# The sine products of the rotary embedding on VectorE: two operations for each projected piece in place of four

## The chip, the cores and the metric

The kernel runs on one core of a Trainium2 chip. A core has a matrix engine (TensorE, PE in the profile), a vector engine (VectorE, DVE), a scalar engine (ScalarE, ACT), GpSimd (POOL) and a queue that issues transfers (SyncE, SP). Each takes its instructions in order, and they wait for each other through semaphores. The metric is the device time of one execution in microseconds; the median of the runs counts.

## The reference

One macaron block on x of shape (8, 512, 512): half a feed-forward part, attention, half a feed-forward part, each on a layer-normalised input and added to x.

```python
x = x + 0.5 * ffn(layernorm(x), router_w, router_b, expert_w, expert_b)
x = x + attn(layernorm(x), Wq, Wk, Wv, Wo, lq1, lq2, lk1, lk2, rms_w)
x = x + 0.5 * ffn(layernorm(x), router_w, router_b, expert_w, expert_b)
# attn: 16 heads of q and 4 of k with 64 values (two halves of 32), v with 32
q = rope(q); k = rope(k)         # re*cos - im*sin, re*sin + im*cos, all 32 pairs of a head
energy = einsum('bqhad,bkhad->bahqk', q, k)      # a: the two halves, causal mask
scores = softmax(energy / sqrt(32))
diff = softmax(scores[:, 0] - lam * scores[:, 1])
att = einsum('bhqv,bvhd->bqhd', diff, v)         # then an rms norm and Wo
# ffn: each of 16 experts takes its 256 best tokens, weighted by the router's softmax
```

## The kernel before

The 4096 rows of x are 32 tiles of 128 rows. The program has three stages: the first feed-forward part (up to about 188 us), the middle with attention (to about 1745 us), and the choice of tokens of the second feed-forward part with the last sum. The change touches only the middle.

In the middle, three kinds of work run side by side. **Preparation** of a tile normalises its rows, turns them, projects them onto q, k and v in three pieces (`project(0)` and `project(1)`, 512 columns of q each, `project(2)`, 256 columns of k and 128 of v), rotates each piece (rope), splits it into two float16 parts and turns these for the energies. **Attention** handles pairs of a head and two row tiles: TensorE computes energies (L1923, mask L1925), VectorE takes each row's bias (`row_bias`, L1214), ScalarE exponentiates (L1670) with row sums, VectorE and GpSimd form the scaled difference (`inv_sums` L1221, `gamma` L1228, `mask` L1510, `scale` L1517, `difference` L1240, `diff_bias` L1249), GpSimd and ScalarE shift it (L1524, L1679), TensorE turns it (`turn_diff`, L1937), ScalarE exponentiates it (`probs`, L1687) and TensorE multiplies it with v (`weigh`, L1955), after which VectorE takes the head's result out (`take_head`, L1260). **After-work** on a tile takes the squares and sums of the heads (GpSimd L1621; VectorE `head_sums`, L1360 to L1367; GpSimd's power `head_root`, L1627), normalises (`head_norm`, L1373), multiplies with Wo and the experts' matrix and stores.

One turn of the middle's loop covers 8 pairs. The first 5 tiles are prepared in a prologue without attention; turns 0 to 26 then prepare tiles 5 to 31, the first five of these (to about 500 us) without after-work; the last five turns (from about 1433 us) have no preparation. `run_bodies` lays the order of each engine out from a table of slots: each turn has 24, three to a step. VectorE does `rope(0)` in slot 5, `rope(1)` in slot 9, `rope(2)` in slot 15; other work of the same engine stands before and behind it in a fixed order.

Rotating one piece is done by `rotate(n, ...)`. The weights' columns were laid out beforehand so that a head of 64 columns is `(a r f)`: two halves `a` of 32, in each 16 real parts and then 16 imaginary parts (`r`), `f` counting them. One operation (L1329) multiplies the piece in PSUM by the cosines into `rot`; four more (L1337), one for each `r` and `a`, multiply the other part of the same half by the signed sines into `rot_t`, which is the tile `scratch`. The last of the four raises `rope_v`. GpSimd waits for it and adds the two (`rope_add`, L1585); ScalarE takes the high float16 part (`rope_high`, L1715), GpSimd the low one (`rope_low`, L1600). TensorE waits for `rope_v` too, before it projects the next piece into the same bank. In the prologue the same `rotate` works on other buffers (`ex`, `df`, `pr`), and the adding is L1556.

Of the kernel before, what the change touches and what calls it, by code (L numbers as in the profile page):

```python
# [15 lines left out]
ALU = mybir.AluOpType  # L16
# [9 lines left out]
P = 128  # L26
B, S, E = 8, 512, 512
H, KVH = 16, 4
D = E // H
# [155 lines left out]
def program(nc, x, wqkv, wo, we, wr, lams, rms, rb, eb, consts, out, x1_d, x2_d, y2_d):  # L185
# [14 lines left out]
    with top:  # L200
# [714 lines left out]
        with ExitStack() as ctx:  # L915
# [285 lines left out]
            def _(dve):  # L1201
# [102 lines left out]
                def first_rope(u, n):  # L1304
                    if u >= 2:
                        rlo_done.wait(dve, 3 * (u - 2) + n)
                    proj_done.wait(dve, 3 * u + n)
                    rotate(n, p_bank(u, n), p_rot[u % 2][n], p_tmp[u % 2][n], u % TB)
# [14 lines left out]
                def rotate(n, bank_, rot_, tmp_, t):  # L1323
                    width = 512 if n < 2 else NK
                    heads = width // (2 * D)
                    src = bank_[:, 0:width]
                    cos = cst[:, ds(t * (2 * D) + C_COS, 2 * D)]
                    sin = cst[:, ds(t * (2 * D) + C_SIN, 2 * D)]
                    dve.tensor_tensor(rot_.rearrange("p (h f) -> p h f", h=heads),  # L1329
                                      src.rearrange("p (h f) -> p h f", h=heads),  # L1330
                                      cos.unsqueeze(1).broadcast_to([P, heads, 2 * D]), ALU.mult)
                    s4 = src.rearrange("p (h a r f) -> p h a r f", h=heads, a=2, r=2)
                    o4 = tmp_.rearrange("p (h a r f) -> p h a r f", h=heads, a=2, r=2)
                    n4 = sin.rearrange("p (a r f) -> p a r f", a=2, r=2)
                    for r in range(2):
                        for a in range(2):
                            ins = dve.tensor_tensor(  # L1337
                                o4[:, :, a, r, :], s4[:, :, a, 1 - r, :],
                                n4[:, a, r, :].unsqueeze(1).broadcast_to([P, heads, D // 2]), ALU.mult)
                    ins.then_inc(rope_v.sem, 1)  # L1340

                def rope(n):

                    width = 512 if n < 2 else NK

                    def f(u, pi):
                        if u is None:
                            return
                        if pi is not None:
                            ss_done.wait(dve, pi)  # L1350
                            dve.wait_ge(y2_st, pi * 16 + 16)
                        proj_done.wait(dve, 3 * u + n)
                        rlo_done.wait(dve, 3 * u + n - 1)
                        rotate(n, project_bank(n), rot[:, 0:width], rot_t[:, 0:width], u & 3)
                    return f
# [901 lines left out]
```

## Time and profile before

| | us |
|---|---|
| median of 3 runs | 1824.33 (1821.73 to 1828.74) |
| the profiled execution | 1832.2 |
| its span, from first to last instruction | 1830.4 |

| engine | busy us | share of the span |
|---|---|---|
| TensorE (matmul) | 1465.6 | 80% |
| VectorE | 1454.8 | 79% |
| ScalarE | 1261.2 | 69% |
| GpSimd | 1084.6 | 59% |

Busy time is a union over overlapping instructions. An instruction's own duration runs from its start to its end, and the next of the same engine may start before that end; so the distance between two starts says what the engine gives to an instruction, and the duration says more than that. The idle time in front of an instruction stands in brackets with what ended it. The profiled execution is 7.9 us above the median of the runs, 0.4%.

### The profile page before, as it was taken

The numbers are of one execution on the slowest core, as the hardware profiler recorded it, in microseconds if no ns is written. First come the engines' busy times: TensorE is split into PE (matmuls) and PEld (weight loads), VectorE is DVE, ScalarE is ACT, GpSimd is POOL, SyncE is SP. The second block draws the span as 40 slices with busy tenths as digits, with TensorE's granted clock in tenths as the row PEclk, the third lists the DMA queues.
The fourth block names the chain that finished last, engine by engine and source line by source line (L and its number), as shares of the span: only waits on it lengthen the run. The fifth ranks groups of instructions, "written<-read, shape, count | busy, mean of one in ns | idle before, by whom it ended". The sixth has DMA issues, their size and how long they took to land. (4 is left out here: it accounts for less than half of the span.)

```text
span 1830.4 us, 43823 instructions
## 1 busy us (share of the span) xinstructions
PE 1465.6 (80%) x10688; PEld 1028.4 (56%) x10688; DVE 1454.8 (79%) x5505; ACT 1261.2 (69%) x3426; POOL 1084.6 (59%) x1493
## 2 busy tenths in 40 slices
PE   3996735988889898988888988888888888888620
PEld 3542313766666666666666666666666666566310
DVE  6778416888898888889988888888989877684477
ACT  2362325787788788878888888878878777675320
POOL 5421534666677777777777777777767666554300
PEclk9998866788899999989999999899989977886855
DMA  8024221111111111111111111111111100001186
GB/s 305 2 64 151 83 68 32 35 36 32 30 46 45 50 44 50 44 44 47 48 44 44 44 44 44 44 44 50 49 45 50 47 22 17 17 23 41 41 314 251
DMA packets 178954, 115.99 MB, mean 63 GB/s; under 512 B 139090, under 2 KB 139474, under 8 KB 178899
## 3 DMA queue, kind: packets, MB, share of 16 engines
q1 hardware_dynamic: 178898, 115.34, 21.4%
q8 instruction: 25, 0.41, 0.1%
q14 instruction: 31, 0.25, 0.0%
HBM read 50.26 MB, written 33.55 MB: 46 GB/s over the span
## 5 line engine op out<-in xcount | busy, mean ns | idle before, releaser
L1670 ACT ACTIVATE ex<-bank,nbias 128x512 f32<-128x512 f32 (+3 forms) x1024 | 528.8, 540 | 80.9 <-DVE bank L1214 78.6
L1214 DVE TENSOR_SCALAR_CACHE_REDUCE bank<-bank,nesc 128x512 f32<-128x512 f32 (+3 forms) x1024 | 503.2, 551 | 88.8 <-PE bank L1925 88.1
L1955 PEld LDWEIGHTS bank<-vs,pr 128*128 128x128 f32 x2560 | 332.8, 205 | 24.3 <-issue 12.3
L1955 PE MATMUL bank<-vs,pr 128*128 (+1 forms) x2560 | 337.6, 283 | 10.2 <-DVE att L1260 5.7
L1937 PE MATMUL bank<-cst,df 128*128 128x128 f32 x1280 | 264.6, 309 | 85.9 <-ACT pr L1687 85.2
L1923 PE MATMUL bank<-ks,hall 96*128 (+2 forms) x1024 | 266.7, 337 | 71.5 <-ACT ex L1670 48.1
L1517 POOL TENSOR_SCALAR ex<-ex,gam 128x128 f32<-128x128 f32 (+3 forms) x512 | 318.7, 635 | 0.0
L1687 ACT ACTIVATE pr<-bank 128x128 f32<-128x128 f32 (+3 forms) x512 | 232.3, 454 | 87.9 <-PE bank L1937 86.8
L1240 DVE CUSTOM_DVE_ANT_0 df<-ex 128x128 f32<-128x128 f32 (+3 forms) x512 | 261.3, 525 | 8.5 <-issue 4.0
L1937 PEld LDWEIGHTS bank<-cst,df 128*128 128x128 f32 x1280 | 168.4, 166 | 114.4 <-ACT pr L1687 99.0
L1670 ACT ACTIVATION_READ_ACCUMULATOR ex<-bank,nbias 128x1 f32 x1024 | 223.8, 219 | 0.0
L1925 PE MATMUL bank<-mask_b,ident_b 128*128 128x128 bf16 x1024 | 210.4, 239 | 0.0
L1923 PEld LDWEIGHTS bank<-ks,hall 96*128 (+1 forms) x1024 | 111.0, 108 | 164.6 <-issue 99.8
L1679 ACT ACTIVATE df<-df,dbias,rsum 128x512 f32<-128x512 f32 (+1 forms) x256 | 201.8, 788 | 0.0
L1524 POOL TENSOR_SCALAR df<-df,rsum,dbias 128x128 f32<-128x128 f32 (+1 forms) x256 | 147.7, 577 | 38.7 <-DVE dbias L1249 38.7
L1600 POOL TENSOR_TENSOR split<-rot,split 128x512 f16<-128x512 f32 (+1 forms) x81 | 80.6, 995 | 112.6 <-ACT split L1715 112.6
L238 PE MATMUL bank<-wqkv_h,b_xt 128*128 128x512 f16 x360 | 142.3, 395 | 3.2 <-ACT turned L1757 1.2
L240 PE MATMUL bank<-wqkv_h,b_xt 128*128 128x512 f16 x360 | 143.6, 399 | 0.0
L239 PE MATMUL bank<-wqkv_l,b_xt 128*128 128x512 f16 x360 | 143.0, 397 | 0.0
L1214 DVE DVE_READ_ACCUMULATOR bank<-bank,nesc 128x1 f32 x1024 | 140.7, 137 | 0.0
L1228 DVE SCALAR_TENSOR_TENSOR gam<-esum,lam,rsum 128x2 f32<-128x2 f32 x256 | 113.6, 444 | 33.7 <-DVE rsum L1221 23.9
L1510 POOL TENSOR_SCALAR_AFFINE_SELECT ex<-ex 128x256 f32<-128x256 f32 x256 | 122.2, 477 | 22.2 <-DVE gam L1228 22.2
(358 smaller groups left out, 2942.1 us busy)
## 6 DMA issues: line engine op xcount, KB each, us to landing
hall<-turned SPq DMA_DIRECT2D x360, 64.0 KB, 2.1
x_dram<-hall SPq DMA_DIRECT2D x8, 1024.0 KB, 4.9
hall<-x_dram SPq DMA_DIRECT2D x8, 1024.0 KB, 14.5
c_y<-y_dram SPq DMA_DIRECT2D x8, 1024.0 KB, 14.5
out_dram<-hall SPq DMA_DIRECT2D x8, 1024.0 KB, 4.7
hall<-in_x SPq DMA_DIRECT2D x7, 1024.0 KB, 13.8
x<-x_dram SPq DMA_DIRECT2D x28, 256.0 KB, 2.7
x_dram<-x SPq DMA_DIRECT2D x28, 256.0 KB, 2.0
```

The source lines that it names most:

```text
L240: mm = eng.matmul(acc, a_lo(k), b_hi(k), start=False, stop=last and k == KT - 1)
L1214: dve.tensor_scalar(part, part, nesc[:, 0:1], None, ALU.mult, ALU.min, accum_out=nbias[:, j, i, a:a + 1]).then_inc(bias_done.sem, 1)
L1240: dve.tensor_tensor_reduce(out=df[j % 4][:, lo:hi], in0=ex[j % 4][:, 0, lo:hi], in1=ex[j % 4][:, 1, lo:hi], scale=1.0, scalar=-3e38, op0=A ...
L1517: gp.tensor_scalar(ex[j % 4][:, 1, lo:hi], ex[j % 4][:, 1, lo:hi], gam[:, j, i:i + 1], 1.0, ALU.mult, ALU.mult).then_inc(scaled.sem, 1)
L1524: gp.tensor_scalar(df[j % 4][:, lo:hi], df[j % 4][:, lo:hi], rsum[:, j, 0, 0:1], dbias[:, j, 0:1], ALU.mult, ALU.add).then_inc(shifted_sho ...
L1670: ac.activation(ex[j % 4][:, a, lo:hi], energy(j, i)[:, a, :], ACT.Exp, bias=nbias[:, j, i, a:a + 1], scale=-1.0, accum_out=esum[:, j, i, ...
L1679: ac.activation(df[j % 4][:, lo:hi], df[j % 4][:, lo:hi], ACT.Identity, bias=dbias[:, j, 1:2], scale=rsum[:, j, 1, 0:1]).then_inc(shifted_ ...
L1687: ac.activation(pr[j % 2][:, lo:hi], bank[:, 6, 0:hi - lo], ACT.Exp).then_inc(prob_done.sem, 1)
L1923: pe.matmul(out_e, q.rearrange("p a n -> p (a n)"), k.rearrange("p a n -> p (a n)"), start=True, stop=True)
L1925: mm = pe.matmul(out_e[:, n - P:n], ident_b[:, :], mask_b[:, :], start=False, stop=True, skip_group_check=True)
L1937: tr = pe.transpose(bank[:, 6, k * P:(k + 1) * P], df[j % 4][:, lo + k * P:lo + (k + 1) * P], ident)
L1955: mm = pe.matmul(bank[:, 7, t * DV:(t + 1) * DV], pr[j % 2][:, lo + k * P:lo + (k + 1) * P], val, start=(k == 0), stop=(k == t))
```

## The change

For each `r` there was one operation for half `a` = 0 and one for `a` = 1. Now one operation takes both: its output and its first input keep the dimension of the halves, and the sines are read as (heads, 2, 16), repeated over the heads.

```diff
                     for r in range(2):
-                        for a in range(2):
-                            ins = dve.tensor_tensor(
-                                o4[:, :, a, r, :], s4[:, :, a, 1 - r, :],
-                                n4[:, a, r, :].unsqueeze(1).broadcast_to([P, heads, D // 2]), ALU.mult)
+                        ins = dve.tensor_tensor(
+                            o4[:, :, :, r, :], s4[:, :, :, 1 - r, :],
+                            n4[:, :, r, :].unsqueeze(1).broadcast_to([P, heads, 2, D // 2]), ALU.mult)
                     ins.then_inc(rope_v.sem, 1)
```

With 8 heads in a piece an operation now has 256 elements for each partition where it had 128; with 4 heads it has 128 where it had 64. Every other instruction stays where it stood in its engine's order. The lines behind L1337 move up by one.

## Rows read from the trace of the kernel before

**Rows 1.** Page, 40 equal slices of the span: busy tenths of two engines.
```profile
PE   3996735988889898988888988888888888888620
...
DVE  6778416888898888889988888888989877684477
```

**Rows 2.** Busy time by stretch: length; PE, PEld, DVE, ACT, POOL; clock, DMA.
```profile
525.30:1405.54 880.24, 788.69 (x6019) 565.68 (x6017) 782.99 (x3063) 729.39 (x2042) 647.14 (x901) 0.93 0.18 46
790.16:834.71 44.55, 39.96 (x304) 28.29 (x303) 38.95 (x154) 36.52 (x103) 32.05 (x46) 0.92 0.19 46
834.71:877.42 42.71, 38.05 (x308) 27.75 (x307) 38.94 (x156) 36.42 (x103) 32.52 (x46) 0.99 0.19 48
```

**Rows 3.** Groups of VectorE by shape, whole span: busy, mean ns, idle before.
```profile
L1337 DVE TENSOR_TENSOR scratch<-bank,cst 128x128 f32<-128x128 f32 x216 | 46.8, 275 | 0.0
...
L1337 DVE TENSOR_TENSOR scratch<-bank,cst 128x64 f32<-128x64 f32 x108 | 16.3, 212 | 0.0
```

**Rows 4.** Timeline of VectorE around two pieces: start, duration, instruction.
```profile
913.63 0.42 DVE L1329 TENSOR_TENSOR rot<-bank,cst 128x256 f32<-128x256 f32 x1
913.97 0.61 DVE L1337 TENSOR_TENSOR scratch<-bank,cst 128x64 f32<-128x64 f32 x4
914.49 0.17 DVE L1221 RECIPROCAL rsum<-esum 128x4 f32<-128x4 f32 x1
...
938.58 0.87 DVE L1337 TENSOR_TENSOR scratch<-bank,cst 128x128 f32<-128x128 f32 x4
939.37 0.74 DVE L1214 TENSOR_SCALAR_CACHE_REDUCE bank<-bank,nesc 128x512 f32<-128x512 f32 x1
```

**Rows 5.** Waits between 525 and 1405 us: total, times, longest.
```profile
DVE bank L1214 <- PE bank L1925: 28.0, 20, 2.1
DVE att L1260 <- PE bank L1955: 25.2, 18, 3.0
...
POOL rot L1585 <- DVE scratch L1337: 35.2, 40, 2.1
```

**Rows 6.** Timeline of the turn from 965 us, rope(0) and what follows.
```profile
975.65 2.92 POOL L1627 TENSOR_TENSOR ast<-ast,half 128x16 f32<-128x16 f32 x1 [2.15 <-DVE ast L1367]
...
980.90 0.87 DVE L1337 TENSOR_TENSOR scratch<-bank,cst 128x128 f32<-128x128 f32 x4
...
984.29 1.27 POOL L1585 TENSOR_TENSOR rot<-rot,scratch 128x512 f32<-128x512 f32 x1
...
985.75 0.62 ACT L1715 CAST split<-rot 128x512 f16<-128x512 f32 x1 [0.90 <-POOL rot L1585]
```

**Rows 7.** The same turn, rope(1), then the next wait of VectorE.
```profile
988.81 0.86 DVE L1337 TENSOR_TENSOR scratch<-bank,cst 128x128 f32<-128x128 f32 x4
...
989.76 1.27 POOL L1585 TENSOR_TENSOR rot<-rot,scratch 128x512 f32<-128x512 f32 x1 [0.33 <-DVE scratch L1337]
...
999.73 0.62 DVE L1214 TENSOR_SCALAR_CACHE_REDUCE bank<-bank,nesc 128x384 f32<-128x384 f32 x1 [2.04 <-PE bank L1925]
```

**Rows 8.** The same turn, rope(2), then the next wait of VectorE.
```profile
1001.96 0.60 DVE L1337 TENSOR_TENSOR scratch<-bank,cst 128x64 f32<-128x64 f32 x4
...
1014.00 0.29 DVE L1260 COPY att<-bank 128x132 f32 x1 [0.87 <-PE bank L1955]
```

**Rows 9.** VectorE in an early turn, and around rope(2) of the turn from 834 us.
```profile
473.39 0.60 DVE L1337 TENSOR_TENSOR scratch<-bank,cst 128x64 f32<-128x64 f32 x4
...
867.93 0.63 DVE L1214 TENSOR_SCALAR_CACHE_REDUCE bank<-bank,nesc 128x384 f32<-128x384 f32 x1 [0.37 <-PE bank L1925]
...
870.15 0.61 DVE L1337 TENSOR_TENSOR scratch<-bank,cst 128x64 f32<-128x64 f32 x4
```

**Rows 10.** Timeline of TensorE in the turn from 965 us.
```profile
988.43 0.33 PE L1937 MATMUL bank<-cst,df 128*128 128x128 f32 x1 [0.50 <-ACT pr L1687]
...
995.79 0.33 PE L240 MATMUL bank<-wqkv_h,b_xt 128*128 128x384 f16 x1
...
996.42 0.53 PE L240 MATMUL bank<-wqkv_h,b_xt 128*128 128x384 f16 x1
```

## What the change does to the time: the prediction

> **What bounds the kernel now.** I read the slices of the page first. In the middle stage both TensorE and VectorE stand at 8 or 9 tenths busy, slice after slice [rows 1], so the slices do not say which of them sets the pace; a change that takes work from VectorE might give all of it or nothing. The busy time by stretch says the same: of 880.2 us that 20 full turns take, TensorE is busy 788.7 and VectorE 783.0 [rows 2]. A turn is 880.2 / 20 = 44.0 us.
>
> The next view is that of the waits in these turns. VectorE does wait: 28.0 us in 20 waits for energies in front of `row_bias`, and 25.2 us in 18 waits for the product with v in front of `take_head` [rows 5]. Both stand once in most turns. Two places a turn where VectorE sits idle until TensorE has something for it mean that time saved ahead of such a place only makes that wait longer, unless TensorE's work itself hung on what VectorE did faster. So the question is not how much VectorE saves but which of the sine products lie on the chain that sets a turn.
>
> For that I went back through a turn from each instruction to what ended last before it: the releaser in brackets where there was idle time, else the instruction in front. In the turn from 965 us the chain goes so: VectorE waits for `weigh`, takes the head out and goes on without a gap to the head sums; these release GpSimd's power L1627 at 975.65, after 2.15 us of idle time of GpSimd; GpSimd then works without a gap until `rope_add(0)` at 984.29, 1.27 us long; ScalarE waits 0.90 us for it [rows 6]; ScalarE's probabilities release TensorE's L1937 at 988.43 [rows 10]; TensorE's product with Wo, its energies, turns, another exchange with ScalarE and the third projection follow, up to the energies that VectorE awaits at 999.73 for 2.04 us [rows 7]. So each of the four engines holds a part of the turn, and VectorE's part is the stretch with the head sums and sometimes that behind 999.73.
>
> **The change part by part.** *What an operation gives back.* The four operations of a piece with 128 elements last 275 ns each by their own durations, those with 64 elements 212 ns [rows 3]. But their starts are closer: four of the larger begin at 938.58 and the next instruction at 939.37, 0.79 us or 0.198 us for one; four of the smaller take 914.49 - 913.97 = 0.52 us, 0.13 each [rows 4]. What VectorE gives to a piece is this distance. From 64 to 128 elements it grows by 0.068 us, or 1.06 ns for an element, and what is left for no elements at all is 0.062 us. Merging two operations saves that constant once.
>
> *What the new ones cost.* The trace of before has no operation of VectorE of just this form, with three dimensions in the sines and 256 elements. The nearest row is the cosine product of the third piece: 256 elements from PSUM, the cosines repeated over four heads; it starts at 913.63 and the next at 913.97, 0.34 us [rows 4]. Two of these are 0.68 us in place of 0.79: 0.11 us saved for a large piece. A small piece becomes two operations of 128 elements, 2 x 0.198 = 0.40 in place of 0.52: 0.12 us saved. I take these values, since rows of 16 elements with a jump between them are already in the old operations, at the same rate as the cosine's plain rows. The lower bound of the cost is the constant taken in full, 2 x 0.062 = 0.124 us saved for each. The upper bound, should a third dimension break the overlap with the next instruction, is the full duration of the cosine product, 0.42 us [rows 4]: 2 x 0.42 = 0.84 in place of 0.79, 0.05 us lost.
>
> There are 32 tiles with two large pieces and one small: 64 x 0.11 + 32 x 0.12 = 10.9 us less work for VectorE in all (from 12 us less to, by the upper bound, about 5 us more).
>
> The Trainium skill weighs an operation higher. In "VectorE: DVE Perf Modes", section "The TRN2 errata — SBUF-src ops pay a fixed extra latency per instruction", a VectorE operation from PSUM costs 120 cycles and one for each element at 0.96 GHz, and many small tiles pay the constant each time. By that estimate each operation left out gives back 125 ns, 250 ns for a piece and 24 us in all. The durations agree with such a constant (275 ns against 258 by the page), the distances between starts do not (62 ns); the same page's section "Two Vector instructions with no wait between them" says that an instruction that is not held starts before the one in front has ended, and the rows show that here. The sum goes by the distances.
>
> *rope(0).* In the full turns its sines start at 980.90 and are over about 0.8 us later. GpSimd, for which they are meant, gets to `rope_add(0)` only at 984.29, having worked without a gap since 975.65 [rows 6]. The sines are early by some 2.6 us, and 0.11 more is nothing. VectorE's own next steps gain 0.11, but run into operands that GpSimd delivers on the same late chain. On the path: 0.
>
> *rope(1).* Its sines do release GpSimd at 989.76 after a wait of 0.33, so `rope_add(1)` starts 0.11 us earlier. What comes of that: VectorE reaches the wait for energies earlier, 2.04 us long in this turn [rows 7], 0.37 in about a third of the turns [rows 9]. Both are longer than 0.11. ScalarE takes the sum up far later, in its own order. On the path: 0; the cover is that wait, and if it were gone this piece would bring 20 x 0.11 = 2.2 us.
>
> *rope(2).* It stands behind the wait for energies, so VectorE is on the path up to there in some turns. In the turn from 965 us it is not: a second wait of 0.87 at 1014.00 follows [rows 8], and TensorE and ScalarE got there by a chain of their own. In others it is: in the turn from 834 us the energies come at 867.93, the sines follow at 870.15 and VectorE goes on without a wait for TensorE to the next head sums [rows 9]. Following the chain back through all 20 turns I find the sines of rope(2) on it 7 times, those of the other two never.
>
> *The early turns and the prologue.* In the five turns without after-work the chain holds less of GpSimd, and 9 of their 15 pieces lie on it, the last at 473.39 [rows 9]; in the prologue one, since ScalarE, GpSimd and later the stacking transfers hold it up. The last five turns rotate nothing.
>
> *The sum.* 7 + 9 + 1 = 17 pieces on the path, 0.12 us each: 2.0 us. The profiled execution of 1832.2 us would become 1830.2; taken off the median of 1824.33, which is 7.9 us below the profiled one, it is 1822.3 us. Bounds of the operation's cost on these 17 pieces: 2.1 us faster to 0.9 us slower.
>
> **The rivals.** *All of VectorE's saving comes through.* VectorE is busy 783.0 of 880.2 us, in a turn at the full clock 38.94 of 42.71 [rows 2], and if it paced every turn the 10.9 us would all be gained: 1813.4 us. For it speaks that in the turns of 42.71 us VectorE waits least. Against it, the two waits for TensorE, 53.2 us in 20 turns, which this rival needs to be on a path that itself shortens.
>
> *The durations are the price.* If an operation's own duration counted, a large piece would go from 4 x 0.275 to 2 x 0.42 us and a small one from 4 x 0.212 to 2 x 0.275: 0.26 and 0.30 us saved, 26 us in all [rows 3, 4]. On the 17 pieces of the path that is 17 x 0.27 = 4.6 us, 1819.7 us; all through, 1798 us. Against it speak the starts in rows 4, in every piece. The Trainium skill's price from the section named above would give 17 x 0.25 = 4.3 us, or 24 us all through.
>
> *TensorE's clock, other side.* TensorE's matmuls in the third projection go from 0.33 to 0.53 us at about 996 us [rows 10], the step from the full clock to the half, and the turn from 790 us, with a mean granted clock of 0.92, takes 44.55 us where that from 834 us, at 0.99, takes 42.71 with the same work [rows 2]. Each turn has short half-clock stretches behind waits of TensorE; a few turns have fewer. The change shifts the instructions by a tenth of a microsecond against these stretches. If each of the 20 turns came out like that of 790 us, it would cost 20 x (44.55 - 44.01) = 10.8 us and use up the saving: 1835.1 us, slower. It decides in the third projection, from the point where TensorE's pause in front of it is followed by the half clock in every turn. *The same with luck:* each turn like the one from 834 us, 20 x (44.01 - 42.71) = 26 us, or 1798 us; half of the turns, 1811.
>
> *The merged operation is slow,* 0.42 us each: 17 x 0.05 = 0.9 us on the path, and at the very most 96 x 0.05 = 4.8 us: 1825 to 1829, no difference that can be seen.
>
> **How the numbers follow.** A measurement of this kernel can tell about 0.5%, 9.1 us, from no change: 1815.2 to 1833.5. Chances: the forecast, 0.71; the durations as the price, but off the path, 0.02; the slow merged operation, 0.05; all through, 0.09; the clock to the good, 0.06; the clock to the bad, 0.07. Faster by over 0.5% are the last but two and the last but one: 0.15. Slower: 0.07. Within: 0.78. The range takes in the first rival (1813) and part of the clock's good case, and reaches up to the spread of the runs of before (4.4 us above the median) and some of the clock's bad case: 1811 to 1832; what it leaves out, the ends of the two clock cases, is about 1 in 10.
>
> **What would show it.** In the profile after: two operations for a piece, about 0.34 us from start to start in the large ones and 0.20 in the small, and VectorE's busy time down by about 11 us; the wait for energies in front of `row_bias` and that in front of `take_head` together longer by about what VectorE saves in the full turns, some 5 us; GpSimd still without a gap from L1627 to `rope_add(0)`; turns of about 44 us, with a mean clock near 0.93. It would be wrong if VectorE's waits stayed as they were and the turns shrank by 0.3 us, or if the clock of the turns moved by some hundredths.

## The result: slower by 0.8% in the first measurement, by 0.3% over three

| | before | after |
|---|---|---|
| median of 4 runs each | 1823.88 us (1821.73 to 1828.74) | 1838.82 us (1835.47 to 1842.12) |
| ratio | | 1.0078, interval 1.005 to 1.0106 |
| profiled execution, its span | 1832.2, 1830.4 us | 1839.7, 1837.9 us |
| VectorE busy | 1454.8 us | 1441.9 us |

The forecast was 1822.3 us, a gain of 2 us too small to be seen, with 1811 to 1832 as its range; the measured median lies above the range, and the change is a small loss. Later sets of executions of the same two kernels give smaller losses: 1.0013 (0.9997 to 1.0028) with 12 of after and 29 of before, and 1.0033 (1.0014 to 1.0053) with 8 and 13. The interval of the first of these includes 1. All three sets together hold 24 executions of after with a mean of 1835.9 us and 46 of before with 1830.7: about 5 us or 0.3%, and 4 us without the first set. Not one of the 24 is below 1830 us; of before 20 of 46 are. The first four of before, with a mean of 1824.6 us, were all among the lower ones of their kind, and the first four of after, with 1838.8, lie above the mean of theirs; so the first measurement shows more than there is. The executions of before in all sets reach from 1819.8 to 1846.4 us, over 26 us, and what spreads them is the thing to explain.

What the change was to do to VectorE it did. The groups of VectorE by shape, whole span of the changed kernel (busy, mean ns, idle before; they answer to [rows 3]):

```profile
L1336 DVE TENSOR_TENSOR scratch<-bank,cst 128x256 f32<-128x256 f32 x108 | 39.9, 408 | 0.0
...
L1336 DVE TENSOR_TENSOR scratch<-bank,cst 128x128 f32<-128x128 f32 x54 | 12.8, 278 | 0.0
```

And its timeline around a large and a small piece (start, duration; they answer to [rows 4]):

```profile
1030.64 0.74 DVE L1336 TENSOR_TENSOR scratch<-bank,cst 128x256 f32<-128x256 f32 x2
1031.30 0.74 DVE L1214 TENSOR_SCALAR_CACHE_REDUCE bank<-bank,nesc 128x512 f32<-128x512 f32 x1
...
1050.01 0.48 DVE L1336 TENSOR_TENSOR scratch<-bank,cst 128x128 f32<-128x128 f32 x2
1050.40 0.17 DVE L1221 RECIPROCAL rsum<-esum 128x4 f32<-128x4 f32 x1
```

A large piece takes 0.66 us from start to start where it took 0.79, a small one 0.39 where it took 0.52. That is 0.13 us for either, 96 x 0.13 = 12.5 us in all, and VectorE's busy time fell by 12.9. The third dimension costs nothing that can be seen here, and over the 20 full turns no other group of VectorE takes more than 0.6 us longer than before.

The time was lost elsewhere. Busy time by stretch, one turn of the changed kernel, then all 20 full ones (length; PE, PEld, DVE, ACT, POOL; granted clock; they answer to [rows 2]):

```profile
1012.77:1057.14 44.37, 39.77 (x304) 28.11 (x303) 38.64 (x150) 36.37 (x103) 31.96 (x46) 0.92 0.18 46
525.13:1412.13 887.00, 794.82 (x6022) 562.72 (x6021) 773.11 (x2943) 727.36 (x2041) 640.07 (x901) 0.92 0.18 46
```

The full turns take 887.0 us in place of 880.2, which is nearly all of the 7.5 us between the two profiled spans. And nearly all of them are alike: from the fourth of the 20 on each takes 44.36 to 44.38 us. In the profile of before they varied from 42.71 [rows 2] to 44.71. TensorE's timeline shows where such a turn spends its clock; 16-bit matmuls of 512 columns in the experts' product of the changed kernel:

```profile
970.92 0.63 PE L238 MATMUL bank<-we_h,at 128*128 128x512 f16 x1
972.20 0.63 PE L238 MATMUL bank<-we_h,at 128*128 128x512 f16 x1
973.22 0.38 PE L238 MATMUL bank<-we_h,at 128*128 128x512 f16 x1
...
1045.51 0.33 PE L240 MATMUL bank<-wqkv_h,b_xt 128*128 128x384 f16 x1
```

Up to 972.2 they last 0.63 us, at half the clock (1.2 GHz), then 0.38, at the full one (2.4 GHz). In these turns the half-clock stretch lies at this place every time, and the third projection (the last line, from the next turn) runs at the full clock. In the turn of before from 965 us it is the other way round: the experts' product runs at the full clock, and the third projection falls to the half [rows 10].

```profile
968.28 0.38 PE L240 MATMUL bank<-we_h,at 128*128 128x512 f16 x1
```

In the changed kernel VectorE then waits for the product with v behind it, 2.98 us in the turn from 1012.77. Waits between 525 and 1412 us, which answer to [rows 5]:

```profile
DVE att L1260 <- PE bank L1954: 56.1, 20, 3.1
...
DVE bank L1214 <- PE bank L1924: 12.8, 20, 2.0
POOL rot L1584 <- DVE scratch L1336: 12.7, 40, 1.8
```

Two waits behind the experts' product grew with it. ScalarE waits for its result 34.6 us in 19 waits, before 7.9 in 5, and GpSimd for the transfer of that result out of `scratch` 38.5 us in 18 waits, before 9.0 in 5.

### The profile page after: what moved, and what is told of

The parts are those of the page before. It is cut to its first block and busy times, and to the rows that moved or that the text cites. A ratio compares the mean times of both kernels' runs of the same rounds, so it can differ in the third digit from the quotient of the medians.

```text
span 1837.9 us, 43581 instructions
## 1 busy us (share of the span) xinstructions
PE 1473.1 (80%) x10688; PEld 1025.9 (56%) x10688; DVE 1441.9 (78%) x5313; ACT 1259.1 (69%) x3426; POOL 1076.3 (59%) x1493
## 5 line engine op out<-in xcount | busy, mean ns | idle before, releaser
L1516 POOL TENSOR_SCALAR ex<-ex,gam 128x128 f32<-128x128 f32 (+3 forms) x512 | 314.6, 625 | 0.0
L1240 DVE CUSTOM_DVE_ANT_0 df<-ex 128x128 f32<-128x128 f32 (+3 forms) x512 | 256.9, 516 | 9.4 <-issue 4.9
L1669 ACT ACTIVATION_READ_ACCUMULATOR ex<-bank,nbias 128x1 f32 x1024 | 228.3, 223 | 0.0
L238 PE MATMUL bank<-wqkv_h,b_xt 128*128 128x512 f16 x360 | 137.9, 383 | 3.0 <-ACT turned L1756 1.2
L239 PE MATMUL bank<-wqkv_l,b_xt 128*128 128x512 f16 x360 | 138.4, 384 | 0.0
L240 PE MATMUL bank<-wqkv_h,b_xt 128*128 128x512 f16 x360 | 137.9, 383 | 0.0
L1509 POOL TENSOR_SCALAR_AFFINE_SELECT ex<-ex 128x256 f32<-128x256 f32 x256 | 118.2, 462 | 22.2 <-DVE gam L1228 22.2
## 6 DMA issues: line engine op xcount, KB each, us to landing
c_y<-y_dram SPq DMA_DIRECT2D x8, 1024.0 KB, 14.6
```

The costliest lines, as they stand in the source:

```text
L239: eng.matmul(acc, a_hi(k), b_lo(k), start=False, stop=False)
L1240: dve.tensor_tensor_reduce(out=df[j % 4][:, lo:hi], in0=ex[j % 4][:, 0, lo:hi], in1=ex[j % 4][:, 1, lo:hi], scale=1.0, scalar=-3e38, op0=A ...
L1516: gp.tensor_scalar(ex[j % 4][:, 1, lo:hi], ex[j % 4][:, 1, lo:hi], gam[:, j, i:i + 1], 1.0, ALU.mult, ALU.mult).then_inc(scaled.sem, 1)
L1669: ac.activation(ex[j % 4][:, a, lo:hi], energy(j, i)[:, a, :], ACT.Exp, bias=nbias[:, j, i, a:a + 1], scale=-1.0, accum_out=esum[:, j, i, ...
```

## The experiments

**Theory A**: what sets a full turn is whether and where TensorE falls to half its clock behind its waits; the change moves the kernel from a mixture of turns, some with hardly any time at half clock, to turns that always have a long stretch of it. **Theory B**: the merged operations meet GpSimd's otherwise and lengthen its chain, or are bad by their form.

### The kernel before once more, and one piece at a time

The unchanged kernel:

> The kernel before, unchanged, once more, for a second profile of it: the one profiled execution of before took 1832.2 us, 8 us above its median, so its pattern of turns may not be the usual one. Theory A (the turns are held at a fixed length by TensorE's half-clock stretch, and before escapes from that in some turns): the same time as before, near 1823 us, and in the profile more turns of about 42.7 us than the 2 of 20 of the first profile, and hardly any run of turns of 44.37 us. Theory B (the merged operations shift VectorE against GpSimd, and GpSimd's own chain gets longer by collisions): the full turns here are all alike and about 0.7 us shorter than the 44.37 us of the changed kernel.

Measured: median 1830.2 us of 10, from 1825.6 to 1839.6; ratio 1.0002 (0.998 to 1.0025). That is 7 us above the 1823 expected: the first executions of before had been unusually quick. Its profiled execution was a quick one, 1825.6 us. Five turns of it in a row, then the 20 full ones:

```profile
877.64:921.40 43.76, 39.01 (x299) 27.97 (x297) 39.66 (x154) 36.41 (x103) 32.36 (x46) 0.92 0.18 46
921.40:965.36 43.96, 39.48 (x302) 28.36 (x301) 39.12 (x154) 36.36 (x103) 31.95 (x46) 0.93 0.18 46
965.36:1009.60 44.24, 39.83 (x304) 28.64 (x303) 39.16 (x154) 36.60 (x103) 32.36 (x46) 0.92 0.18 46
1009.60:1053.43 43.83, 39.34 (x302) 28.28 (x301) 39.03 (x156) 36.23 (x103) 32.44 (x46) 0.93 0.18 46
1053.43:1096.09 42.66, 38.04 (x308) 27.77 (x307) 38.91 (x154) 36.41 (x103) 32.42 (x46) 0.99 0.19 48
528.92:1402.26 873.34, 782.32 (x6019) 563.74 (x6017) 783.74 (x3061) 728.24 (x2042) 646.15 (x901) 0.94 0.18 47
```

This pattern of five repeats through the whole stage, with four turns of 42.7 us, and the 20 turns take 873.3 us. The first profile of the kernel before had taken 880.2 with two such short turns. So one kernel, unchanged, has several patterns, and an execution falls into one of them: the two profiles of before lie 6.6 us apart, nearly as far as before and after.

For the three pieces the operations were merged in one of them only, in the loop, with the prologue as before:

```diff
-                    for r in range(2):
-                        for a in range(2):
+                    if not early and n == 0:          # 1 and 2 in the other two kernels
+                        for r in range(2):
+                            ...                       # one operation
+                    else:
+                        for r in range(2):
+                            for a in range(2):
```

> Of the change only the merged sines of the first piece, rope(0), in the loop; prologue and the other pieces as before. Its sines are over 2.6 us before GpSimd adds them. Theory A: any shift of a tenth of a microsecond may change the pattern, so each piece alone can come out anywhere between 1818 and 1840 us, with turns of 44.37 us wherever it is slow. Theory B: a piece that is early for GpSimd anyway does nothing, 1822 to 1825 us.

Measured: 1829.8 us (1823.6 to 1840.3), ratio 1.0003 (0.9982 to 1.0024); the profiled execution of 1840.3 us had its turns held at 44.37.

> Only rope(1) merged, in the loop. Theory A: between 1818 and 1840 us, slow only with turns of 44.37 us. Theory B: rope_add(1) starts 0.11 us earlier and may meet GpSimd and VectorE otherwise; if the loss comes from here alone, 1835 us or more, and the sum of the three pieces' effects is the whole change's 15 us.

Measured: 1830.9 us (1821.3 to 1834.6), ratio 1.0007 (0.9991 to 1.0024); the profiled execution of 1821.3 us had four of 20 turns below 43 us.

> Only rope(2) merged, in the loop. Theory A: between 1818 and 1840 us, slow only with turns of 44.37 us, and the three pieces' effects do not add up to the whole change's 15 us. Theory B: they add up; this one is the piece on the path in 7 of 20 turns, so 1 to 2 us faster if no collision comes of it.

Measured: 1830.6 us (1827.4 to 1835.2), ratio 1.0002 (0.9981 to 1.0023). None of the three can be told from the kernel before. That speaks against one piece that carries the 15 us of the first measurement; but each interval is some 4 us wide to either side, so a third of a loss of 5 us in each piece would not be seen. The runs also show that one profile of such a kernel says little: the three fell into three different patterns. One turn of each of the first two, at the same place:

```profile
1013.13:1057.49 44.36, 39.79 (x303) 28.12 (x302) 38.92 (x154) 36.38 (x103) 31.97 (x46) 0.92 0.18 46
```
```profile
963.42:1006.05 42.63, 38.01 (x308) 27.75 (x307) 38.79 (x152) 36.38 (x103) 32.39 (x46) 0.99 0.19 48
```

### More and less work for VectorE

The changed kernel again, beside many executions of before:

> The changed kernel, unchanged, once more beside many runs of the kernel before. Executions of before now spread from 1824 to 1841 us, and profiled ones show two patterns of turns: a held one (every turn 44.37 us, one long half-clock stretch in each) and a mixed one (42.7 to 44.2 us). Theory A1 (the change makes the held pattern more likely): the ratio stays near 1.008, and most executions lie at 1835 to 1842 us with a mean clock of 0.861 to 0.864. Theory A2 (the pattern is drawn anew in every execution, the first measurement of four runs drew badly): a ratio within 0.997 to 1.003, with executions from 1824 to 1842 us.

Measured: 1833.9 us of 12 (1830.8 to 1839.5), ratio 1.0013 (0.9997 to 1.0028), before 1823.9 to 1842.2. Between A1 and A2: the median is 3.4 us higher and the quick executions are missing. In its profile no turn of the 20 is below 43.97 us.

```diff
                     n4 = sin.rearrange("p (a r f) -> p a r f", a=2, r=2)
+                    dve.tensor_reduce(pad[:, n:n + 1], cst[:, 0:64], X, ALU.max)
```

> The merged sines, and before them in each piece one small operation of VectorE (a maximum over 64 constants, written to a tile that nobody reads) that gives back the 0.12 us saved. Nothing of the computation is left out. Theory A1, by timing: like the kernel before, ratio 1.000. If the form of the merged operation did harm by itself: like the changed kernel, 1.008. Theory A2: 1.000 within 0.3%.

Measured: 1831.7 us of 11 (1826.2 to 1845.1), ratio 0.9998 (0.9979 to 1.0018). With the time given back the quick executions are there again: 4 of 11 below 1830 us, where the changed kernel has none in 24. That speaks for the timing and against the form of the merged operation, though not alone: e6 and e5 lie 2 us apart, and their intervals overlap.

```diff
-                    for r in range(2):
+                    for r in range(parts):            # 1 in the loop, 2 in the prologue
```

> In the loop only the first of the two merged sine products of a piece; the other, half of the sine products, is left out (the tile is zeroed once, so that half of it holds old values). VectorE saves another 0.34 us for a large piece and 0.20 for a small one, 0.9 us a turn, three times what the change saves. If VectorE's work on these pieces were on the path, 27 turns x 1.2 us = 32 us faster than before; by the reading of the prediction (17 pieces on the path, 0.45 us) 7 us faster, 1816 to 1823 us against before's 1823 to 1830. Theory A1: any value down to 1815 or up to 1840 us, by the share of turns held at 44.37 us.

Measured: 1837.1 us (1830.1 to 1841.3), ratio 1.0027 (1.0011 to 1.0043). By the sum of the expectation VectorE has some 24 us less to do than in the changed kernel; the kernel is not faster than that one, and slower than before. Two of its turns:

```profile
877.94:922.44 44.50, 39.80 (x303) 28.64 (x302) 38.58 (x145) 36.55 (x103) 32.57 (x46) 0.92 0.18 46
922.44:966.64 44.20, 39.66 (x303) 28.54 (x302) 38.38 (x147) 36.44 (x103) 32.64 (x46) 0.92 0.18 46
```

These two lengths alternate for the most part, 44.2 and 44.5, with the clock at 0.92: a pattern of its own, without a short turn. That time saved on these pieces comes through as a whole is ruled out.

VectorE's busy time in a turn hardly fell (38.4 and 38.6 us against 38.8 in e5), though 0.9 us of work was gone. Groups of VectorE between 530 and 1400 us show why, in e5 and then in e7:

```profile
L1228 DVE SCALAR_TENSOR_TENSOR gam<-esum,lam,rsum 128x2 f32<-128x2 f32 x157 | 77.5, 493 | 24.1 <-DVE rsum L1221 18.7
...
L1240 DVE CUSTOM_DVE_ANT_0 df<-ex 128x384 f32<-128x384 f32 x79 | 46.4, 588 | 0.0
L1240 DVE CUSTOM_DVE_ANT_0 df<-ex 128x256 f32<-128x256 f32 x79 | 33.1, 419 | 3.5 <-issue 3.5
```
```profile
L1241 DVE CUSTOM_DVE_ANT_0 df<-ex 128x384 f32<-128x384 f32 x79 | 67.7, 856 | 0.0
...
L1229 DVE SCALAR_TENSOR_TENSOR gam<-esum,lam,rsum 128x2 f32<-128x2 f32 x157 | 54.3, 346 | 21.8 <-DVE rsum L1222 16.3
L1241 DVE CUSTOM_DVE_ANT_0 df<-ex 128x256 f32<-128x256 f32 x79 | 43.5, 550 | 3.5 <-issue 3.5
```

Between 530 and 1400 us the sine products take 17 us less. The differences take more, 0.86 us on average in place of 0.59 with 384 elements and 0.55 in place of 0.42 with 256, in all four lengths 33.5 us; gamma takes less, 0.35 in place of 0.49, 23.2 us in all. So 10 of the 17 us come back as longer instructions. Both kinds read two operands from SBUF. Gamma visibly lasts until GpSimd is done: in the turn of [rows 7] it ran from 989.91 to 991.04, GpSimd's addition from 989.76 to 991.03, and of gamma's 160 executions in the full turns of before all 42 that last over 0.6 us end with an instruction of GpSimd, to within 0.03 us. So part of the time that VectorE gains is spent inside a later instruction that lasts until GpSimd has finished, where it counts as busy. That the differences stretch for the same reason was not checked.

```diff
                     n4 = sin.rearrange("p (a r f) -> p a r f", a=2, r=2)
+                    dve.tensor_reduce(pad[:, 2 * n:2 * n + 1], cst[:, 0:64], X, ALU.max)
+                    dve.tensor_reduce(pad[:, 2 * n + 1:2 * n + 2], cst[:, 0:64], X, ALU.max)
```

> The kernel before with two small operations of VectorE more in each piece (maxima over 64 constants, written to a tile that nobody reads), about 0.25 us a piece, 0.75 us a turn. If VectorE were on the path: 27 x 0.75 = 20 us slower. By the reading of the prediction: 17 pieces x 0.25 = 4 us slower, since the waits for the energies and for the product with v take the rest. Theory A1: not in line with the sum, faster than before if the turns fall out of the held pattern.

Measured: 1846.3 us of 4 (1842.3 to 1851.5), ratio 1.009 (1.0068 to 1.0112). Slower, by 16 us where the reading by waits gave 4 and full exposure 20. In its profile, of 1842.3 us, the 20 full turns take 882.1 us, no more than in other executions; three of the early turns take 44.4 where they took 41.1 to 41.3, and the full turns start 14 us later than in the profile of before. One of these early turns, and its counterpart in the kernel before:

```profile
405.52:449.92 44.40, 40.83 (x250) 30.20 (x249) 34.72 (x150) 33.09 (x98) 26.18 (x41) 0.73 0.15 28
```
```profile
398.41:439.57 41.16, 35.03 (x251) 26.02 (x250) 34.14 (x146) 33.17 (x98) 26.00 (x41) 0.88 0.13 30
```

The time is lost where the clock is lost, 0.73 in place of 0.88, with VectorE only 0.6 us busier; so this run does not show what VectorE's work costs by itself.

### TensorE kept at work in front of its waits

The decisive test gives TensorE more to do. Behind the energies of each pair, and behind its product with v, come some short matmuls of constants into the PSUM bank that is free at that time; they lie in front of waits for ScalarE.

```diff
+                def keep_warm(j, count):
+                    free = (3, 2, 1, 0)[j % 4]
+                    for _ in range(count):
+                        pe.matmul(bank[:, free, 0:P], ident_b[:, :], ones_b[:, :], start=True, stop=True)
...
                         mm.then_inc(e_done.sem, 1)
+                        if i == 0:
+                            exp_done.wait(pe, at.units(4, -1))
+                            keep_warm(j, 4)
...
                     mm.then_inc(av_done.sem, 1)
+                    keep_warm(j, 4)
```

> The kernel before, with TensorE kept at work in front of its waits for ScalarE: four short matmuls of constants (128 columns) behind the energies of each pair and four behind its product with v, into a PSUM bank that is free there, 64 in a turn, about 3.5 us of TensorE's time by the 0.055 us that a matmul of 128 columns in 16 bits takes from start to start at the full clock; TensorE stands idle for 4.5 us of a turn. They change no result. Theory A (the turns are held near 44.4 us by half-clock stretches that follow TensorE's waits): the mean clock of the full turns rises from 0.92 to 0.97 or more and they get shorter, 43 us or less, in spite of more work for TensorE; 1800 to 1825 us. If the clock is only a bystander: TensorE's added work lengthens the turns by 1 to 3 us each, 1850 us or more.

Measured: 1796.9 us (1795.5 to 1798.8), ratio 0.9822 (0.9754 to 0.989); before 1825.6. More work for TensorE makes the kernel 29 us faster, more than expected. The matmuls came with one more wait of TensorE for ScalarE in each pair; e11 below has that wait too and no gain, so it is not the wait. One of its turns and all 20:

```profile
864.20:906.52 42.32, 39.78 (x365) 30.12 (x366) 39.41 (x156) 36.42 (x103) 32.36 (x46) 1.00 0.19 48
...
524.10:1372.11 848.01, 796.78 (x7290) 603.54 (x7309) 787.91 (x3061) 728.47 (x2041) 647.52 (x901) 1.00 0.19 48
```

> The same added matmuls in the changed kernel. Theory A: where the clock stays up, the merged sines are worth what the prediction said, 2 us less than the same matmuls in the kernel before (e9), at most 11; the difference between e9 and e10 is then no loss. If the merging does harm by itself, e10 is 3 to 15 us slower than e9.

Measured: 1801.3 us (1798.6 to 1805.5), ratio 0.985 (0.978 to 0.992). It is 4.3 us slower than e9, which by the expectation speaks for a harm of the merging by itself; its turns say what that harm is:

```profile
864.81:908.86 44.05, 41.22 (x374) 31.34 (x373) 39.08 (x150) 36.58 (x103) 31.96 (x46) 0.97 0.18 46
908.86:951.07 42.21, 39.74 (x367) 30.09 (x366) 39.05 (x150) 36.28 (x103) 32.36 (x46) 1.00 0.19 48
...
1035.46:1079.51 44.05, 41.22 (x373) 31.32 (x373) 39.07 (x148) 36.58 (x103) 31.96 (x46) 0.97 0.18 46
523.51:1376.76 853.25, 802.11 (x7284) 607.06 (x7302) 780.94 (x2941) 727.09 (x2041) 645.24 (x901) 0.99 0.19 48
```

This pair of runs shows the whole case in small. At the full clock a turn takes 42.20 us with the merged sines and 42.33 without: one piece's 0.13 us of the three does come through. But with them every fourth turn has a half-clock stretch and takes 44.05 us, 1.85 more. Three turns win 0.13 each, the fourth loses 1.7: over 20 turns 853.3 us against 848.0. A turn that is a tenth of a microsecond shorter meets the drops of the clock otherwise, and one drop costs fourteen times what the edit saves in a turn.

> The kernel before with two short matmuls at each of these places, 32 in a turn, 1.8 us of TensorE's time. Theory A: the clock rises less than with four (0.93 to 0.97), and the time lies between before and e9. If the clock is a bystander: half of e9's loss.

Measured: 1830.5 us (1825.8 to 1836.2), ratio 1.0016 (0.9978 to 1.0053). No gain, and neither the loss of a bystander clock nor the part of the gain that A expected: three of its full turns take 42.2 us, and the last 14 are held at 44.37 with a clock of 0.92. The changed kernel, e2 and e6 are held at the same length, with other work in the turn.

```profile
962.85:1007.22 44.37, 41.24 (x335) 30.07 (x334) 39.00 (x156) 36.40 (x103) 32.37 (x46) 0.92 0.18 46
```

> The kernel before with six short matmuls of constants at each of the two places of a pair, 96 in a turn, 5.3 us of TensorE's time. No half-clock stretch in the 20 full turns. The turns get longer than the 42.33 us with four where the matmuls no longer fit into TensorE's waits: 42.3 to 44 us, 1797 to 1830 us.

Measured: 1798.5 us (1796.7 to 1801.4), ratio 0.9818 (0.9767 to 0.9868). Two of the 20 full turns still hold a half-clock stretch and take 44.4 us, where none was expected; the others take 42.7 to 42.8.

> The same in the changed kernel. If the merged sines are worth their time wherever the clock stays up: no half-clock stretch in the full turns, each of them up to 0.13 us shorter than in e12, and 0 to 5 us less in all. If something else in the merged operations costs time: e13 slower than e12 by 2 us or more with the same clock.

Measured: 1787.5 us of 4 (1783.9 to 1794.9), ratio 0.9754 (0.9696 to 0.9811): the fastest kernel of the study, 45 us below before in the same set of runs, and 11 below e12, where 0 to 5 were expected. Turns of e12 and of e13:

```profile
736.09:778.83 42.74, 40.90 (x398) 31.81 (x398) 39.14 (x154) 36.31 (x103) 32.36 (x46) 1.00 0.18 48
```
```profile
729.42:772.16 42.74, 40.91 (x398) 31.84 (x398) 38.73 (x150) 36.28 (x104) 32.42 (x46) 1.00 0.19 48
```

At the full clock the turns are equal, 42.74 us; TensorE, busy 40.9 of them, now sets them, and the 0.4 us less of VectorE (39.14 and 38.73 busy) bring nothing. So the 11 us are not the saving in these turns. The two profiled executions lie 6.1 us apart: the early turns end 6.7 us earlier in e13, its full turns take 3.2 us longer, 861.5 against 858.3, since four of them hold a half-clock stretch where two do in e12, and what follows them is 3 us shorter. In turns at the full clock the merged sines do no harm, 42.74 against 42.74 here and 42.20 against 42.33 in e10 and e9; how much of the 11 us is the edit and how much the pattern of the stretches, four executions do not tell.

> The changed kernel with five matmuls at each place, between e10 and e13. By the clock alone: the half-clock stretch of every fourth turn in e10 is gone and the turns stay near 42.2 to 42.6 us, so 1792 to 1800 us, 3 to 8 us faster than e10. If one more matmul at each place costs more than it keeps: 1801 us or more.

Measured: 1798.2 us (1797.8 to 1800.5), ratio 0.9815 (0.9765 to 0.9865). As expected by the clock: one half-clock turn in 20, the others 42.45 us.

> The changed kernel with eight matmuls behind the energies of each pair and none behind its product with v: 64 in a turn as in e10, at one place in two. If the amount decides: turns and time as in e10, 1799 to 1805 us. If the place decides: half-clock stretches in most turns again, 1815 us or more.

Measured: 1827.9 us of 10 (1813.1 to 1837.3), ratio 0.9974 (0.9942 to 1.0005). The same 64 matmuls a turn as in e10, 27 us slower: the amount alone does not decide, the place does too. Of its 20 full turns eight take 42.7 to 42.95 us and twelve 44.33 to 44.38.

> The changed kernel once more, to settle the size of the loss. If the first measurement of four executions was a bad draw from the patterns of turns: a ratio of 1.000 to 1.003, as in e5, with a profiled execution whose turns of 42.7 us are few or none. If the loss is 15 us: 1.006 or more.

Measured: 1836.4 us of 8 (1831.7 to 1844.8), ratio 1.0033 (1.0014 to 1.0053), with one turn of 42.9 us in the profile. Smaller than the first measurement's 1.0078, larger than e5's and just above the 1.000 to 1.003 expected; the intervals of the first and of e5 do not meet, so an interval from a few executions of one set is narrower here than the kernel's own variety.

With this profile there are three of the changed kernel and two of the kernel before. The record of the granted clock in the traces, added up over the 20 full turns, gives this (us):

| profiled execution | the 20 full turns | of that at half clock | full turns less half of it |
|---|---|---|---|
| e1, kernel before | 873.3 | 108.8 | 818.9 |
| first profile of before | 880.2 | 122.4 | 819.0 |
| e16, changed kernel | 883.4 | 129.0 | 818.9 |
| e5, changed kernel | 886.8 | 135.8 | 818.9 |
| first profile of after | 887.0 | 136.1 | 819.0 |

Each microsecond at half clock costs half a microsecond, with the merged sines or without, and nothing else tells these five apart, to within 0.2 us: in the full turns the loss is half-clock time, and the saving for VectorE does not show. The kernels e2, e3, e4, e6, e7 and e8 give 818.1 to 820.0 in the last column. It is an account and not a forecast for a kernel without half-clock time: e9, with its added matmuls, has hardly any and takes 848.0.

Whole executions point the same way less sharply. In the 109 executions of before that have a mean granted clock on record, the time is 1.7 us longer for each 0.001 of clock less (correlation -0.88). The 24 of the changed kernel have a mean clock of 0.8658 against 0.8679, worth 3.5 of the 5.1 us between the two means; the other 1.6 us are not explained. And not all of the spread lies in the full turns: the profiled execution of e16, the slowest of the changed kernel at 1844.8 us, has the shortest full turns of its three and starts them 8.4 us later than the first profile of before.

## Why the prediction was wrong, step by step

- **Price of an operation: right.** 0.13 us a piece measured, 0.11 to 0.12 taken, 0.124 as the lower bound. VectorE's busy time fell by 12.9 us where 11 was said. The estimate of 250 ns a piece from the Trainium skill ("VectorE: DVE Perf Modes", section "The TRN2 errata — SBUF-src ops pay a fixed extra latency per instruction") was not seen.
- **What lies on the path: right in kind.** Of the three pieces of a turn at most one is on it: 0.13 us a turn in e9 against e10, where the prediction had 7 x 0.12 over 20 turns at the mixed clock. Without added matmuls even those 0.8 us do not show in the table above. e7 shows that three times the saving gains nothing either.
- **The waits in front of `row_bias` and `take_head`** grew together from 53.2 to 68.9 us, by 15.7, not by 5: VectorE's saving in 20 turns (20 x 3 x 0.13 = 8) and the 6.8 us by which the turns are longer make 14.6 of it. The prediction named them as the place; it left out the second part.
- **GpSimd's chain** from the power to `rope_add(0)` is without a gap as before (981.02 to 989.65 in the turn from 968 us); no collision was added there. With the equal or shorter turns at the full clock in e10 and e13, theory B falls.
- **The step that failed** is the one that is not in the sum: that the mean turn of 44.0 us would stay but for the pieces on the path: a change of half-clock time stands at nothing in the sum, without a reason. Turns with a granted clock of 0.92 and of 0.99 stood side by side in the rows, and the prediction gave the case in which all come out like the slow kind 0.07, with 10.8 us as its price. That is what happened, at 44.37 us where it took 44.55: in the profiled pair 136.1 us at half clock in place of 122.4, and full turns longer by 6.8 us. No row said what held the kernel in its mixture, so the case deserved more than 0.07; and one profiled execution, itself 8 us above its median, could not say what the usual mixture was.
- **The place was wrong too.** The prediction let the third projection decide. In the held turns that runs at the full clock, and the half-clock stretch lies in the experts' product. So it did already in the turn of before from 790 us, where those matmuls last 0.63 us from 791.42 on and those of the third projection 0.33; it is the turn whose 44.55 us the prediction took as the price.
- **How far the number was off** is luck in good part. Of the 16.5 us between the forecast and the measured median, 6.4 are the base: 1824.3 us, where the 46 executions of before in the three sets have a mean of 1830.7. Another 2.9 us are the first four of after against their own mean of 1835.9. The 7.2 us left are the forecast gain of 2 and the real loss of 5.
- **The range** was too narrow at the top for the same reason: executions of the kernel before alone reach from 1819.8 to 1846.4 us, where the first three spanned 7.

The Trainium skill, in "TensorE: Matmul & The Clock Gate", part 1, section "What's actually happening", says that the array's clock follows how busy TensorE has lately been. Runs e9 and e12 to e14 agree: matmuls of constants in front of the waits bring the granted clock of the full turns from 0.93 to 0.99 or 1.00. A higher clock does not always pay: in e11 and e15 the full turns have 0.94 and 0.98, and the time stays that of before.

What stays open: why turns of 42.7 us are so rare after the change, one in the 60 full turns of three profiles against six in 40 before, and why quick executions come back with 0.13 us of filler in each piece. The runs show that they do, and that the lengths are held; the exact moment at which the clock decides was not taken from any row. Nor was it tried where between e10's and e15's places the effect lies.

## What to carry to other kernels

A tenth of a microsecond saved on an engine that waits anyway can cost more than it could ever bring if TensorE hovers between its two clocks: look at turns of the loop one by one, and where equal work takes two lengths with two mean clocks, price the clock before the edit. In such a kernel several executions of before, profiled, are worth more than one in every detail. And keeping TensorE at work in front of its waits, at the right places, brought 24 to 45 us here, where all the merged sines together are 12.5 us of VectorE's time.

## What the hardware showed that was not expected

- Turns of four kernels with different work (the changed one, e2, e6, e11) are held at the same 44.37 us, over 14 to 17 turns, to within 0.04 us.
- 64 added matmuls a turn, 3.5 us of TensorE's time by the estimate, shortened the mean full turn from 43.7 or 44.0 to 42.4 us; the same 64 at one place of the two, in the changed kernel, from 44.35 to 43.7 only.
- In full turns without added matmuls each microsecond at half clock made them half a microsecond longer, in five profiles of two kernels to within 0.2 us.
- Gamma, an operation of VectorE on two SBUF tiles, lasts until GpSimd is done: all 42 of its executions over 0.6 us in the full turns of before end with an instruction of GpSimd. The same difference of 384 elements takes 0.59 us on average in e5 and 0.86 in e7.
- An operation of VectorE with three dimensions in one operand, 16 elements in the innermost, runs at the rate of a plainer one: 0.33 us from start to start for 256 elements, where the cosine product takes 0.34 [rows 4].
